# Cross-attention and routed experts on one core: filling turns and last turns in an order of their own, row table ahead of the step tables

## The chip, the cores and the metric

One core of a Trainium2 chip runs the whole program. The metric is the device time in microseconds (us) of one execution. The granted clock is that of TensorE: 1.0 is 2.4 GHz, 0.5 is 1.2 GHz.

## What is computed

There are 16 batches of 128 tokens with 512 numbers each. The attention treats a batch as 128 channels by 512 positions: 8 heads of 16 channels, rotary positions on queries and keys, and a context of the same shape.

```python
x = x + xattn(layernorm(x), ctx)      # q, k, v = W @ inp + b; rotary on q, k
                                      # softmax(q k^T / 4) v; W_o @ out + b_o
t = layernorm(x).reshape(2048, 512)
w, e = top_k(t @ gate_w.T, 8)         # 32 experts, softmax over the 8 chosen
g, u = t @ w_gate_proj[e].T, t @ w_up_proj[e].T       # 192 wide
x = x + sum_k softmax(w)_k * (silu(g) * u) @ w_down_proj[e].T
```

## The kernel before

**Two phases.** The first is a chain of turns, n from -5 to 19, one for each step of a software pipeline over the batches; the second is a loop of up to 160 expert steps, each for one tile of 128 chosen tokens of one expert. Between them VectorE computes a plan of the steps.

**A turn** (`batch_turns`, `turn` of each engine) works on several batches at once: `bl` = n+4 is normalised, `bq` = n+3 gets its projections and rotary positions, `b1` = n+1 its scores for the row maxima, `b2` = n its scores, exponentials and value products, `bo` = n-1 its output and residual, `br` = n-2 its second normalisation, the logits and the choice of experts, and `bs` = n-3 has its rows scattered into the table `expert_rows` in memory. Every engine runs its own list in order, with semaphores between them. Turns -3 to -1 are the filling turns; no batch is in its exponentials yet. In turns 15 and 16 the last two batches drain.

**The way of one batch before its scores.** VectorE takes the statistics (L908 to L914: statistics, aggregation, addition of EPS), GpSimd the power and the shift (L581, L584), ScalarE the normalised x (L731), TensorE four projections in fp32, two records each (L1210 to L1217). VectorE multiplies one pair with the cosines (L905), ScalarE reads the turned pair (L701), GpSimd multiplies it with the sines and adds (L588, L602). ScalarE writes the high fp16 half (L665), GpSimd the low one (L527). SP stores both to memory and loads them back stacked; TensorE's scores for maxima (L1381) and VectorE's maxima, 16 a batch (L899), follow.

**The end of a batch.** ScalarE reads the value products into `o_raw`, in which some rows are the denominators. SP stores these, loads them as 128x32, VectorE inverts them (L919), SP stores them and loads them back spread over the rows, GpSimd multiplies (L595), TensorE makes the output product (L1228), and VectorE adds the residual (L1013).

**The choice of experts.** TensorE's logits (L1247) go to a PSUM bank; VectorE copies them scaled (L939), takes the eight highest (L952), their indices (L957) and casts these (L958), compares them with all expert numbers (L962), sums to a mask (L969), writes weights and token numbers (L977, L978), counts the token number on (L980), and computes the places of the rows (L988 to L998). GpSimd scatters eight rows' columns a batch (L543).

**Banks.** Two pairs of PSUM banks are shared in turn by `m0`, `qk`, `m1` to `m8`, `lg`, `m9` to `m15`, `y` and `cnt`: who comes two places later waits for the one before (`bank_is_free`). The bank of `lg` goes to `m10`.

**Between the phases.** VectorE's plan (L1078 on) gives the step table after 40 instructions; its prefix sum over experts is eleven of them. SP stores and loads the step table, then the table of adds, then waits for the scatters and loads the row table. GpSimd writes four small transfers (L616), waits for the table of adds and starts gathering tokens (L633). ScalarE copies the row numbers (`g_idx`). The first experts' weights are split into halves by `first_weights` in turn 17.

## Time and profile before

| | us |
|---|---|
| median of 3 runs | 1184.73 (1184.3 to 1190.09) |
| the profiled execution | 1200.81 |
| its span, first to last instruction | 1199.0 |

| engine | busy us | share of the span |
|---|---|---|
| TensorE (PE) | 1019.9 | 85% |
| VectorE (DVE) | 726.0 | 61% |
| ScalarE (ACT) | 774.1 | 65% |
| GpSimd (POOL) | 761.8 | 64% |

The span is one execution as the hardware profiler took it, and what lies around it makes the execution's own time. Shares are means over stages with different limits: the rows further down cut the span into stages. PEld is TensorE's weight load, and a name with q (SPq, POOLq) is an engine's queue. An instruction's idle time before it is followed by what ended it.

### The profile page before, as it was taken

What the parts mean: (1) busy time and instruction counts of PE and PEld (TensorE: products, weight loads), DVE (VectorE), ACT (ScalarE), POOL (GpSimd) and SP (SyncE); (2) the same over time, 40 slices, a digit from 0 to 9 for tenths busy, and PEclk for the clock granted to TensorE, in tenths of its full rate; (3) what the DMA queues carried; (4) which work ended last, traced back from release to release, by engine and by line L of the source; (5) the groups of instructions that cost most, each with busy time, mean ns of one, the idle gap of its engine ahead of it and who ended that gap; (6) DMA issues with size and microseconds to landing.
All of it is one profiled execution on the core that took longest, in us unless ns stands there. A gap on an engine that the chain in (4) does not pass through costs nothing.

```text
span 1199.0 us, 29221 instructions
## 1 busy us (share of the span) xinstructions
PE 1019.9 (85%) x6948; PEld 482.1 (40%) x6949; DVE 726.0 (61%) x1453; ACT 774.1 (65%) x1806; POOL 761.8 (64%) x652
## 2 busy tenths in 40 slices
PE   3588998888888898884139999999999999999996
PEld 1222222222222221221026555566566566556663
DVE  2578889989999897862535354554444455444421
ACT  1268878777787785664127666666666676666674
POOL 4523466666666665434656777676777777777776
PEclk8679999999999997887569999999999999999998
DMA  4433434333333332431056878898788898888674
GB/s 138 119 89 112 138 85 121 117 106 116 117 117 116 100 103 77 117 104 34 19 187 156 220 196 213 185 226 213 177 213 212 209 229 196 209 218 203 140 140 89
DMA packets 89700, 176.09 MB, mean 147 GB/s; under 512 B 24340, under 2 KB 41108, under 8 KB 85414
## 3 DMA queue, kind: packets, MB, share of 16 engines
q0 software_dynamic: 38080, 75.58, 29.7%
q1 hardware_dynamic: 51556, 99.80, 26.6%
q8 instruction: 25, 0.41, 0.1%
q14 instruction: 35, 0.29, 0.1%
q10 hardware_dynamic: 4, 0.02, 0.0%
HBM read 118.78 MB, written 61.65 MB: 150 GB/s over the span
## 4 chain that ended last, share of the span: by engine, by line
PE 40%; DVE 21%; issue 15%; DVEq 6%; ACT 6%; ACTq 3%; POOL 2%; DMA 1%; another core or an unknown queue 1%; SPq 0%; POOLq 0%
PE ps L1409 10%; DVE mx L899 10%; PE ps L1370 6%; PE ps L1381 4%; PE ps L1358 4%; DVEq L340 4%; ACTq L340 2%; PE ps L1417 2%; PE ps L1228 2%; DVE w_lo L1159 2%; PE ps L1222 1%; ACT o_raw L665 1%; ACT pr L675 1%; DVE w_hi L1154 1%; POOL expert_rows L543 1%
## 5 line engine op out<-in xcount | busy, mean ns | idle before, releaser
L899 DVE TENSOR_REDUCE mx<-ps 128x2 f32<-128x1024 f32 x256 | 303.3, 1222 | 36.4 <-PE ps L1381 32.9
L675 ACT ACTIVATE pr<-ps 128x512 f32<-128x512 f32 x512 | 279.0, 600 | 63.7 <-PE ps L1358 51.0
L1409 PE MATMUL ps<-w_hi,o_raw 128*128 x1200 | 317.5, 326 | 2.3 <-DVE rope_b L1171 1.8
L649 POOL DMA_INDIRECT out<-v,s_idx x148 | 254.8, 1722 | 100.7 <-issue 43.1
L633 POOL DMA_INDIRECT pr<-normalised_tokens,g_idx x155 | 168.3, 1086 | 58.7 <-issue 24.0
L1409 PE MATMUL ps<-w_lo,o_raw 128*128 x600 | 195.8, 326 | 0.0
L665 ACT ACTIVATE o_raw<-ps 128x1024 f16<-128x1024 f16 (+1 forms) x183 | 175.8, 961 | 2.9 <-PE ps L1370 1.9
L1409 PEld LDWEIGHTS ps<-w_hi,o_raw 128*128 128x128 f16 x1200 | 117.5, 98 | 89.7 <-issue 6.0
L543 POOL DMA_INDIRECT expert_rows<-rows,rowi x128 | 127.3, 995 | 34.7 <-issue 33.1
L1171 DVE SCALAR_TENSOR_TENSOR rope_b<-rope_a,stacks,ps 128x192 f32<-128x192 f32 x150 | 61.8, 412 | 141.6 <-ACT rope_a L787 83.4
L1176 DVE TENSOR_TENSOR rope_s<-rope_b,rope_s 128x128 f16<-128x128 f32 x149 | 43.5, 292 | 170.3 <-issue 115.3
L1370 PE MATMUL ps<-pr,v 128*32 128x512 f32 x1024 | 142.8, 631 | 0.7 <-ACT pr L675 0.6
L1358 PE MATMUL ps<-stacks 49*128 49x512 f16 x512 | 125.7, 398 | 19.7 <-ACT pr L675 15.2
L1381 PE MATMUL ps<-stacks 48*128 48x512 f16 x512 | 107.2, 405 | 38.3 <-DVE mx L899 26.4
L1417 PE MATMUL ps<-ch,pr 128*128 128x128 f16 x1208 | 92.8, 220 | 30.4 <-DMA pr<-normalised_tokens,g_idx 27.9
L581 POOL TENSOR_TENSOR rstd<-vare,cf 128x1 f32<-128x1 f32 x32 | 19.2, 599 | 139.9 <-DVE vare L914 137.8
L787 ACT ACTIVATE rope_a<-ps 128x192 f32<-128x192 f32 x150 | 50.0, 333 | 86.8 <-issue 66.5
L665 ACT ACTIVATE v<-ps 128x512 f32<-128x512 f32 x164 | 98.6, 601 | 8.4 <-PE ps L1222 6.1
L1417 PEld LDWEIGHTS ps<-ch,pr 128*128 128x128 f16 x1208 | 79.7, 98 | 52.1 <-issue 34.1
L1159 DVE SCALAR_TENSOR_TENSOR w_lo<-stage,w_hi x155 | 95.9, 683 | 0.1
L665 ACT ACTIVATE rope_s<-rope_b 128x192 f16<-128x192 f32 x149 | 55.4, 372 | 62.5 <-DVE rope_b L1171 53.3
L665 ACT ACTIVATE x<-ps 128x384 f16<-128x384 f16 x148 | 73.2, 494 | 34.6 <-remote 23.4
(161 smaller groups left out, 1508.8 us busy)
## 6 DMA issues: line engine op xcount, KB each, us to landing
stage<-in_expert_w SPq DMA_DIRECT2D x32, 1280.0 KB
stacks<-qk_parts SPq DMA_DIRECT2D x128, 96.0 KB
w_lo<-in_x SPq DMA_DIRECT2D x32, 256.0 KB, 2.8
w_lo<-in_ctx SPq DMA_DIRECT2D x32, 256.0 KB
qk_parts<-qk SPq DMA_DIRECT2D x32, 256.0 KB
qk_parts<-qk SPq DMA_DIRECT2D x32, 128.0 KB
out<-x SPq DMA_DIRECT2D x16, 256.0 KB
normalised_tokens<-x2s SPq DMA_DIRECT2D x16, 256.0 KB
```

The costliest lines, as they stand in the source:

```text
L543: nc.gpsimd.indirect_dma_start(rows_d, bass.IndirectOffsetOnAxis(rowi[:, b.slot(2), k:k + 1], 0), rows[:, b.slot(2), k, :], None).then_inc ...
L633: nc.gpsimd.indirect_dma_start(xg[:, r, :], None, tok_d, bass.IndirectOffsetOnAxis(g_idx[:, r, 0:1], 0)).then_inc(gathered[r], 16)
L649: nc.gpsimd.indirect_dma_start(out_rows, bass.IndirectOffsetOnAxis(s_idx[:, s.slot(4), 0:1], 0), y_sb[:, s.slot(4), :], None, bounds_check ...
L665: copy = lambda o, i, s=1.0: nc.scalar.activation(o, i, ACT.Copy, scale=s)
L675: nc.scalar.activation(pr[:, n % 8, :], bank(f"s{n}"), ACT.Exp, scale=DH ** -0.5).then_inc(exp_done, 1)
L899: V.tensor_reduce(mx[:, b.slot(2), at:at + 3:2, tile], bank(f"m{n}"), AXX, ALU.max).then_inc(mx_done, 1)
L1159: lo = V.scalar_tensor_tensor(w_lo[:, bass.ds(at_slot + at, LO_PIECE)], stage[:, bass.ds(at_src + at, LO_PIECE)], WSCALE, w_hi[:, bass.ds( ...
L1358: mm(bank(f"s{n}"), k_st[rows_of, b.slot(2), p, sc * P:(sc + 1) * P], q_st[rows_of, b.slot(2), p, :], start=True, stop=True).then_inc(s2_m ...
L1370: last = mm(ps_o[2 * DH * i:2 * DH * (i + 1), :], v1[:, b.slot(2), k % NSC, head, :], pr[:, (4 * k + i) % 8, :], start=(k % NSC == 0), sto ...
L1381: last = mm(bank(f"m{n}")[:, side, :], q_st[rows_of, b.slot(2), p, i * P:(i + 1) * P], k_st[rows_of, b.slot(2), p, :], start=True, stop=True)
L1409: last = mm(ps[:, s.slot(2), 0:2 * INTER], xt[:, s.slot(2), at:at + P], w[:, cols], start=(m == 0), stop=(m == 3 * KT - 1))
L1417: last = nc.tensor.transpose(ps[:, 2 + s.slot(2), :].bitcast(F16)[:, n * P:(n + 1) * P], xg[:, s.slot(GROUP), n * P:(n + 1) * P], ident)
```

## The change

**Loads.** x of batch 0 and the projection weights are SP's first transfers; the other constants follow in turns -4 and -3 with semaphores of their own (`proj_in`, `turn_in`, `consts_in`). The rest of the setup on VectorE, and the bias product on TensorE, move into turn -3. TensorE multiplies zeros 12 times first.

**Filling turns** have lists of their own. In them VectorE makes the whole rotary step and the low halves (`first_rope`, `first_low`) in place of ScalarE's reading, GpSimd's four operations and its two subtractions; ScalarE normalises first. GpSimd stores the empty row table in turn -2 in place of the start, and issues its four small transfers at the start.

**All turns.** The addition of EPS moves to GpSimd, with a constant of its own for the power. The logits are read in PSUM, without a copy; the index search and its cast stand ahead of maximum 9, and `lg_done`, which frees the bank, follows the index search. The token numbers come from a constant table.

**Turns 15 and 16** have lists of their own. The denominators of batches 14 and 15 are spread over the rows by a product with a selecting matrix (`sums`), inverted as 128x512 and multiplied by VectorE (`over_sums`). `first_weights` follows in turn 16, behind the places of batch 14.

**Between the phases.** The prefix sum is one scan. SP waits for the scatters and loads the first part of the row table ahead of the step table and the table of adds, and the rest of it when four gathers have landed. GpSimd waits for the step table ahead of its gathers and for the table of adds ahead of its first add.

```diff
+                if turn_no == -5:
+                    load_x(bi)
+                    sp.dma_start(pw[:, :, :], proj_w).then_inc(proj_in, 16)
+                    return
+                if turn_no == -4:
+                    load_c(bl)
+                    sp.dma_start(pb[:, :], proj_b).then_inc(turn_in, 16)
+                    sp.dma_start(cf[:, :], const_f).then_inc(turn_in, 16)
+                    load_x(bi)
+                    return
+                if turn_no == -3:
+                    load_c(bl)
+                    rest_of_consts()
+                    load_x(bi)
+                    store_stack(bq, 0)
+                    store_stack(bq, 1)
...
+            for p in range(2):
+                sp.wait_ge(rows_stored[p], 16 * TOPK * (NB // 2))
+            sp.wait_ge(s1_mm, 16 * NB)
+            sp.wait_ge(s2_mm, 32 * NB)
+            table = rows_d[0:E * EROWS, :].rearrange("(p r) f -> p (r f)", p=P)
+            first = FIRST_EXPERTS * TILES * 4
+            sp.dma_start(place_of[:, 0:first], table[:, 0:first]).then_inc(first_rows_in, 16)
...
+            for r in range(AHEAD - LEAD):
+                sp.wait_ge(gathered[r], 16)
...
+                if turn_no == NB - 1:
+                    normalised_x2(br)
+                    low_of_x2(br)
+                    scatter_rows(bs, (0, 1, 2))
+                    normalised_x2(bo)
+                    scatter_rows(bs, (3, 4, 5, 6, 7))
+                    low_of_x2(bo)
+                    scatter_rows(br, (0, 1, 2, 3, 4, 5, 6, 7))
+                    return
...
+                if turn_no == NB:
+                    normalised_x2(bo)
+                    scatter_rows(br, (0,))
+                    low_of_x2(bo)
+                    scatter_rows(br, (1, 2, 3, 4, 5, 6, 7))
+                    scatter_rows(bo, (0, 1, 2, 3, 4, 5, 6, 7))
+                    return
...
+                nc.gpsimd.tensor_scalar(vare[:, norm:norm + 1], mv[:, norm, 1:2], EPS, None, ALU.add).then_inc(vare_done[norm], 1)
+                gp.wait_ge(vare_done[norm], b.count(1, 1))
+                apart(gp)
+                nc.gpsimd.tensor_tensor(rstd[:, norm:norm + 1], vare[:, norm:norm + 1], half[:, :], ALU.pow).then_inc(rstd_done, 1)
...
+            gp.wait_ge(tab_in, 16)
...
+                    if bl.live():
+                        normal_x()
+                    if bq.live():
+                        high_of_qk(bq, 0)
+                        high_of_qk(bq, 1)
+                    if b1.live():
+                        read_v(b1)
+                        max_row(b1, 0)
+                    return
...
+            def first_rope(b, w):
+                dve.wait_ge(turn_mm, b.count(2, w + 1))
+                need(dve, rope_sum, b.count(2, w - 1))
+                V.scalar_tensor_tensor(rope_b[:, w, :], bank("kr" if w else "qr"), pb[:, 2 * w + 1:2 * w + 2], cf[:, SIN:SIN + T], ALU.add, ALU.mult).then_inc(turned, 1)
+                dve.wait_ge(rope_done, b.count(2, w + 1))
+                dve.wait_ge(turned, b.count(2, w + 1))
+                need(dve, qk_lo, b.count(2, w - 1))
+                V.tensor_tensor(rope_s[:, w, :], rope_a[:, w, :], rope_b[:, w, :], ALU.add).then_inc(rope_sum, 1)
+            def first_low(b, w):
+                dve.wait_ge(qk_hi, b.count(2, w + 1))
+                need(dve, stack_stored[w], b.count(32, 0))
+                V.tensor_tensor(qk[:, 2 * w + LO, :], rope_s[:, w, :], qk[:, 2 * w + HI, :], ALU.subtract).then_inc(qk_lo, 1)
...
+                link(V.max(top[:, :], bank("lg")[:, 0, 0:E]))
+                V.tensor_scalar(ntop[:, :], top[:, 0:1], -1.0 / WSCALE, None, ALU.mult).then_inc(ntop_done, 1)
+                return link
+            def highest_index(b, link):
+                V.max_index(topi[:, :], top[:, :], bank("lg")[:, 0, 0:E]).then_inc(lg_done, 1)
                 dve.wait_ge(lg_done, b.count(1, 1))
-                apart(dve)
-                link(V.max(top[:, :], lg[:, :]))
-                V.tensor_scalar(ntop[:, :], top[:, 0:1], -1.0, None, ALU.mult).then_inc(ntop_done, 1)
-                return link
-
-            def highest_index(b, link):
-                link(V.max_index(topi[:, :], top[:, :], lg[:, :]))
                 link(V.tensor_copy(topf[:, :], topi[:, :]))
...
+            def over_sums(b, g):
+                n = 2 * (b.count(1) - NB + 2) + g + 1
+                dve.wait_ge(sums_mm, n)
+                dve.wait_ge(on_done, 2 * (NB - 2))
+                V.reciprocal(rcb[:, g, :], v_bank[1][:, g, :]).then_inc(over_done, 1)
+                dve.wait_ge(over_done, n)
+                need(dve, y_mm, b.count(1))
+                V.tensor_tensor(o_n[:, g, :], o_raw[:, b.slot(2), g, :], rcb[:, g, :], ALU.mult).then_inc(on_done, 1)
...
+                if turn_no == NB - 1:
+                    over_sums(bo, 0)
+                    over_sums(bo, 1)
+                    residual(bo)
+                    stats_of_x2(bo)
+                    link = choice(br)
+                    weights(br, link)
+                    read_counts(br)
+                    places(br, link)
+                    over_sums(bo + 1, 0)
+                    return
...
+                if turn_no == NB:
+                    over_sums(bo, 1)
+                    link = choice(br)
+                    residual(bo)
+                    stats_of_x2(bo)
+                    weights(br, link)
+                    read_counts(br)
+                    places(br, link)
+                    first_weights()
+                    return
...
+                    if bq.live():
+                        rope(bq, 0)
+                        rope(bq, 1)
+                        first_rope(bq, 0)
+                        first_rope(bq, 1)
+                    if it.count(1) == -1:
+                        maxima(0, 4)
+                    if bq.live():
+                        first_low(bq, 0)
+                        first_low(bq, 1)
+                    if it.count(1) == -FILL:
+                        rest_of_setup()
+                    if it.count(1) == -1:
+                        maxima(4, 12)
+                    return
...
+            link(V.tensor_tensor_scan(first_step, n_tiles, zero_per_expert, 0.0, ALU.add, ALU.add))
...
+            def sums(b, g):
+                pe.wait_ge(mx_done, 16 * NB)
+                pe.wait_ge(cnt_done, b.count(2, -2))
+                pe.wait_ge(on_done, b.count(2, g - 1))
+                pe.wait_ge(o_read, b.count(2, g + 1))
+                mm(v_bank[1][:, g, :], cf[:, SUMS:SUMS + P], o_raw[:, b.slot(2), g, :], start=True, stop=True).then_inc(sums_mm, 1)
...
+                    s(0)
+                    pv(7)
+                    s(2)
+                    sums(bo, 0)
+                    s(4)
+                    pv(0)
+                    s(6)
+                    sums(bo, 1)
+                    s(8)
+                    pv(1)
+                    s(10)
+                    s(12)
+                    pe.wait_ge(lg_done, NB - 3)
+                    pe.wait_ge(mx_done, 16 * NB)
+                    pe.wait_ge(x2_done, NB - 2)
+                    output(bo)
+                    bank_is_free(pe, it, "xt")
+                    tokens_transposed(br)
+                    pv(2)
+                    s(14)
+                    pe.wait_ge(x2_done, NB - 1)
+                    logits(br)
...
+                if turn_no == NB:
+                    pv(7)
+                    bank_is_free(pe, it, "xt")
+                    tokens_transposed(br)
+                    sums(bo, 1)
+                    pe.wait_ge(lg_done, NB - 2)
+                    logits(br)
+                    bank_is_free(pe, it, "y")
+                    output(bo)
+                    bank_is_free(pe, it, "cnt")
+                    counts_of(br)
+                    return
```

## Rows read from the trace of the kernel before

**Rows 1.** The page's first line.

```profile
span 1199.0 us, 29221 instructions
```

**Rows 2.** Windows by stage: busy us (instructions) per engine, granted clock, DMA share, GB/s.

```profile
0.00:65.14 65.14, 29.82 (x69) 10.83 (x70) 29.50 (x45) 12.77 (x20) 28.89 (x34) 0.75 0.40 125
158.08:435.71 277.63, 242.31 (x1547) 72.09 (x1546) 251.24 (x404) 215.90 (x422) 184.49 (x188) 0.99 0.39 113
524.95:553.87 28.92, 22.92 (x127) 5.75 (x125) 6.50 (x27) 20.58 (x40) 12.31 (x13) 0.82 0.15 45
553.87:619.74 65.87, 8.01 (x60) 4.09 (x58) 32.76 (x118) 8.55 (x17) 40.23 (x41) 0.56 0.21 68
619.74:1199.00 579.26, 553.00 (x4192) 342.61 (x4192) 258.37 (x658) 383.19 (x1046) 419.19 (x299) 0.99 0.80 193
```

**Rows 3.** Timeline of the filling turns: start us, length us, engine, line [idle before <-releaser].

```profile
13.98 2.04 PE L1210 MATMUL ps<-xn,pw 128*128 128x512 f32 x2 [5.82 <-ACT xn L731]
26.78 2.04 PE L1210 MATMUL ps<-xn,pw 128*128 128x512 f32 x2 [6.72 <-issue]
...
44.45 1.22 DVE L899 TENSOR_REDUCE mx<-ps 128x2 f32<-128x1024 f32 x1
```

**Rows 4.** Groups of the first 65.14 us: busy us, mean ns, idle before.

```profile
L908 DVE BATCH_NORM_STATS2 stat<-w_lo 128x6 f32<-128x512 f32 x4 | 2.8, 694 | 24.0 <-DMA w_lo<-in_x 24.0
```

**Rows 5.** Timeline of VectorE in turn 9.

```profile
360.89 0.83 DVE L958 CAST topf<-topi 128x8 f32<-128x8 uint32 x1
371.29 0.15 DVE L914 TENSOR_SCALAR vare<-mv 128x1 f32<-128x1 f32 x1
```

**Rows 6.** Groups of nine steady turns; last row: comparison over the whole run, ns min/median/max.

```profile
L1381 PE MATMUL ps<-stacks 48*128 48x512 f16 x288 | 57.8, 386 | 20.4 <-DVE mx L899 12.2 <-issue 6.2 <-DVE lg L939 0.9
L962 DVE TENSOR_TENSOR chosen<-cf,topf 128x256 f32<-128x256 f32 x9 | 9.4, 1040 | 0.3
L958 DVE CAST topf<-topi 128x8 f32<-128x8 uint32 x9 | 6.4, 711 | 0.3
L962 DVE TENSOR_TENSOR chosen<-cf,topf x16: 424/878/1451, 144.6 to 590.4; 128x256 f32<-128x256 f32 x16
```

**Rows 7.** Window of 5 us in turn 13, columns as in rows 2.

```profile
470.00:475.00 5.00, 4.96 (x19) 0.81 (x19) 2.28 (x2) 2.35 (x5) 3.92 (x5) 0.50 0.28 79
```

**Rows 8.** Timeline of the drain; then power and scatters over the whole run.

```profile
559.24 0.35 DVE L919 RECIPROCAL rcp<-den 128x32 f32<-128x32 f32 x1 [1.65 <-DMA den<-denominators]
575.47 0.69 DVE L1013 TENSOR_TENSOR x<-ps,w_lo 128x512 f32<-128x512 f32 x1 [8.15 <-PE ps L1228]
581.23 2.36 POOL L584 TENSOR_SCALAR shift<-mv,rstd 128x1 f32<-128x1 f32 x1 [0.21 <-POOL rstd L581]
580.63 2.83 DVE L924 SCALAR_TENSOR_TENSOR w_lo<-stage,w_hi 128x2560 f16<-128x2560 f32 x1
593.71 0.17 DVE L998 SCALAR_TENSOR_TENSOR rowi<-topi,at_part 128x8 uint32<-128x8 uint32 x1
600.12 0.38 SPq L477 DMA_DIRECT2D step_table<-stepi  x1
602.05 0.25 SPq L479 DMA_DIRECT2D tab<-step_table  x1
607.18 1.63 POOL L543 DMA_INDIRECT expert_rows<-rows,rowi  x1 [0.30 <-issue]
609.20 2.13 POOL L616 DMA_DIRECT2D started_out<-started  x4 [0.29 <-issue]
610.07 0.34 SPq L507 DMA_DIRECT2D stacks<-expert_rows  x1
619.74 1.86 PE L1417 MATMUL ps<-ch,pr 128*128 128x128 f16 x16 [27.92 <-DMA pr<-normalised_tokens,g_idx]
L581 POOL TENSOR_TENSOR rstd<-vare,cf x32: 549/555/1862, 12.0 to 579.2; 128x1 f32<-128x1 f32 x32
L543 POOL DMA_INDIRECT expert_rows<-rows,rowi x128 | 127.3, 995 | 34.7 <-issue 33.1
```

321 lines of the change are left out of this document (228 added, 93 removed).

## The prediction

> **What bounds the kernel now.** I read the page's first lines first, then the busy time of each engine in stretches cut at the joints of the program, then the groups of the steady turns, and last the timelines around the joints. The profiled execution took 1200.81 us, its span 1199.0 us [rows 1]; the median of the three runs is 1184.73 us, 16 us less. The sum is made against 1200.81 and its difference in us is carried over to the median, since most of the 16 us can lie in the expert steps, which this change leaves alone.
>
> The stretches [rows 2] show three regimes. Up to 65.14 us, where turn 0 starts, no engine is busy half of the time: latency. From 158.08 to 435.71 us lie nine turns of 30.85 us with VectorE at 90% and TensorE at 87%: two engines that wait for each other. From 553.87, where the last value product starts, to 619.74, where the first expert tile is transposed, TensorE works 8 of 66 us: latency again. Then 579 us of expert steps with TensorE at 95%, the same instructions in both kernels. So the change can pay in a fill of 65 us, in 13 steady turns and in a drain of 95 us (turn 15 starts at 524.95).
>
> **The fill, part by part.** VectorE's first work waits for x, which is queued behind the seven constants; it is idle 24.0 us there in total before its statistics [rows 4]. The first projection starts at 13.98 and the second at 26.78 [rows 3]: one turn of the fill costs 12.8 us, because ScalarE's next normalisation stands behind the high halves in its list, and these wait for GpSimd's four rope operations. Turn -1's first maximum starts at 44.45 [rows 3]; sixteen of them, two ropes (1.4) and a stall at the value projection take until 65.14, so 19.3 us without the ropes.
>
> After: x comes first. Statistics can start at about 4 us, but GpSimd now has its fills and the four small transfers ahead (2.13 us for the four [rows 8], which left the drain), so it can answer at about 6.4 us. With the variance, the power and the shift 1.6 us (two short operations, a power of 0.555 [rows 8] and the waits), ScalarE's 0.8 us: first projection at about 9, a gain of 5. The twelve products on zeros lie ahead of it while TensorE waits anyway: no cost. Then VectorE alone carries a turn: statistics 1.1 us and eight operations of 512 columns at 0.69 (the residual add is such a one [rows 8]) with short waits, 7.1 us in place of 12.8. Constants must land for the first rope (x, weights, context and the large table, about 1.5 MB; 5 to 10 us would do it), so turn -3 starts on VectorE near 10, is over with the setup at 18, turn -2 at 25, the ropes of turn -1 at 31 to 32. The sixteen maxima with their stall are 19.3 us as today, the two subtractions among them 1.4: turn 0 at 52, 13 us earlier. Bounds: 8 (constants late, cold projections) and 17. GpSimd's row table fill waits until turn -2 and has all turns to land: nothing.
>
> **The steady turns.** Four instructions leave VectorE's list per turn. The two additions of EPS take 0.15 each [rows 5], 0.22 with the wait, and go to GpSimd, in front of the power; GpSimd is busy 184 of 278 us [rows 2]. ScalarE waits for that chain behind the statistics, so it grows by about 0.25 us, which the shorter list ahead of the statistics gives back. The copy of the logits and the token counter are instructions of the same size as the additions, 0.2 to 0.3 each with their waits. All of this lies around a turn's joint, where TensorE is the later of the two in most turns: I take nothing for it, and at most 1.2 a turn.
>
> What is on the path is the place between maxima 12 and 13: TensorE waits for VectorE's maxima 12.2 us in these nine turns [rows 6]. There the index search (two short instructions, 0.3), its cast (mean 0.711) and the comparison with all experts (mean 1.040, at its shortest 0.424) run one behind the other [rows 6]. The cast took 0.83 at 360.89 [rows 5]; both are long because GpSimd multiplies and subtracts at that time. Search and cast move ahead of maximum 9, beside GpSimd's scatters, where VectorE waits for TensorE in many turns. That takes out about 1.0. Two things give back. The comparison now starts earlier and can meet the GpSimd operation that the cast met: plus 0.2. And the logits' bank is given free after the search instead of after the copy, about 0.6 later; maximum 10's products stand next in TensorE's list and scores and value products behind them. Today TensorE waits there 0.9 us in nine turns for the copy [rows 6]. Plus 0.2, at most 0.6. Net 0.6 a turn, times 13: **8 us**; ends 1 (bank hold at its full price) and 18 (everything counts).
>
> Beside it, a rule. The comparison's long form shows two engines excluding each other: 1.040 in the mean against 0.424. The Trainium skill, page "SBUF — State Buffer", section "Who interferes with whom", has it that an instruction of VectorE with two SBUF inputs, or in a two-port mode, and a GpSimd instruction that reads SBUF lock each other out for a whole instruction. It speaks for the cast's move, and against the place of the first weights' split below. The trace agrees: the power, 0.555 in the median, took 1.862 once, beside the split [rows 8]. If the two did not exclude each other, the drain below would be 3 us shorter.
>
> **The last turns.** Batches 14 and 15 lose the way through memory for the denominators (store, load, reciprocal, store, broadcast) and GpSimd's two multiplications; the residual add of batch 15 starts at 575.47, after VectorE waited 8.15 us for the output product [rows 8], 21.6 after the last value product. New: per half a product with a selecting matrix (1 us, 2 at the lower clock), a reciprocal over 128x512 and a multiplication (0.69). No row has such a reciprocal; the one of 32 columns takes 0.35 [rows 8] and a short instruction of one column 0.15 [rows 5], so 6.2 ns a column and 3.3 us here, as an estimate. Between 0.7 (if it ran like the add) and 5.6 (0.35 times 16). It is on the path once, for batch 15's second half.
>
> From turn 15's start: turn 15 stays at 29 us (three products more on TensorE, fewer waits of ScalarE); VectorE is free in it, busy 6.5 of 28.9 [rows 2]. The second half's sums at +32.4, reciprocal to +35.7, multiplication to +36.4, output product at the lower clock 3.7, residual at about +40.3. Before: 575.47, that is +50.5 [rows 8]. 10 us won. Then statistics, GpSimd's chain, ScalarE's normalisation and high half until +45. GpSimd has one scatter of batch 14 first, which waits for VectorE's places (+44.3), and then the low half. Directly behind the places VectorE splits the first weights (its second half takes 2.83 [rows 8], the first about half of that). Before, that split met the power (1.862 in place of 0.555) and the shift (2.36) [rows 8]. Now it meets the scatter and the low half: I take the same 3 us, so the way from the residual to the last batch's places, 18.2 us today (575.47 to 593.71 [rows 8]), loses only the copy and the counter and some waits, 1.5. Places at +57 instead of +68.8: 12 us. The low half lies about 7 us ahead of them (transposes, copy, logits, choice, counts), at +50.
>
> GpSimd is then the end: today its last scatter starts at 607.18 [rows 8], +82.2. Now 15 scatters follow the low half, each 1.27 from start to start ((127.3 + 34.7) / 128 [rows 8]); the last starts at +67.7: 14.5 won. The plan's scan saves over a microsecond in VectorE's list and nothing on the path. After the scatter lands (2.9), SP loads the row table (610.07 today [rows 8]) and **only then** stores and loads the step table, which took 1.93 from the store's issue to the load's [rows 8] and as much again to land. The order turns: today the step table is in long before the row table, in the new order it comes 1.5 us after it. Against that, the rest of the row table and the weights wait until four gathers have landed, which today share the queues with the first gather: from the row table's load to the first tile are 9.7 us [rows 8], and I take 2 off. The two cancel: first tile at about +80, before +94.8. Drain: **15 us**, ends 6 and 21. What is late next: the rest of the row table, needed from tile 8 on by ScalarE; it lands about when it is asked for, 0 to 2 us.
>
> **Sum.** 13 + 8 + 15 = 36: 1200.8 becomes 1165, the median 1149.
>
> **Rivals.** (1) The turns don't move: the logits' bank costs what the cast's move gives. For it: TensorE is as full as VectorE there. Then 13 + 0 + 14: 1157. (2) The turns take the whole of VectorE's saving, 1.4 a turn, and the fill its upper end: 16 + 18 + 16 = 50: 1135. For it: 12.2 us of waits for maxima. (3) The drain gives only 6, because the split blocks GpSimd's scatters one by one or the step table comes 4 us behind, the fill 10: 10 + 7 + 6 = 23: 1162. (4) The new arrangement of the filling turns does nothing, as the constants come too late for the first rope: fill 4, total 27: 1158. (5) Slower: TensorE's clock. In turn 13, behind a gap in TensorE's work at the turn's start, the granted clock is 0.50 (1.2 GHz) though TensorE is busy 4.96 of 5 us [rows 7]; ten such us cost up to 5, since they hold 5 us of work at the full clock. GpSimd's longer chain sits at just that gap. If it made all 13 turns like this, at 3.5 us each, 46 us would be lost against the 28 won in the fill and the drain: 1203. It decides from 2.2 us a turn. Against it: nine turns run at 0.99 with ScalarE already waiting there.
>
> **Chances.** Forecast 0.52 (own range 1142 to 1156), (1) 0.16, (2) 0.12, (3) 0.08, (4) 0.09, (5) 0.03. The range of 8 in 10 leaves out (5) and the far end of (2) and (3): 1132 to 1165. What a measurement can tell from no change is about 0.5%, 6 us; all cases but (5) lie beyond: faster 0.95, same 0.02, slower 0.03.
>
> **What would show it.** Turn 0's first product at 52 (wrong at 58 or more); distance of turns 30.2 (wrong at 30.8 or under 29.6); in place of 12.2 us of waits for maxima about 7; a new wait of TensorE for the index search; reciprocals of 3.3 us; the low half of the last batch stretched by the split; first tile 80 us after turn 15's start; the expert steps within 4 us of 579.

## Result and profile after

| | before | after |
|---|---|---|
| median (lowest to highest), us | 1187.06 (1184.3 to 1190.09) | 1146.78 (1143.28 to 1158.52) |
| ratio after/before, 95% interval | | 0.9677 (0.96 to 0.9755) |
| profiled execution: time, span, us | 1200.8, 1199.0 | 1158.52, 1156.7 |

The medians differ by 40 us, the profiled spans by 42; 36 were forecast. The prediction, 1149 us, is 2 us above the median; its parts are less exact than its sum. Every stage below is held against one profile of the kernel before, whose execution (1200.8 us) lies 11 us above the longest of its timed runs.

Windows of the changed kernel, columns as in [rows 2]: fill, nine steady turns, turn 15, the rest of the drain, expert steps.

```profile
0.00:52.46 52.46, 30.50 (x82) 10.82 (x83) 40.81 (x59) 9.20 (x14) 10.41 (x26) 0.75 0.54 177
136.94:406.55 269.61, 242.85 (x1551) 71.65 (x1550) 248.39 (x371) 213.88 (x423) 188.80 (x206) 0.97 0.39 115
496.65:532.05 35.40, 28.53 (x133) 7.20 (x131) 19.95 (x38) 21.67 (x42) 16.37 (x21) 0.75 0.15 51
532.05:586.36 54.31, 9.94 (x58) 4.56 (x59) 31.32 (x94) 7.11 (x15) 28.13 (x27) 0.53 0.09 23
586.36:1156.70 570.34, 550.71 (x4192) 341.66 (x4192) 258.16 (x658) 383.23 (x1046) 422.00 (x301) 0.99 0.82 200
```

| stage, us | forecast change | before | after | change |
|---|---|---|---|---|
| start to turn 0's first product | -13 | 65.1 | 52.5 | -12.7 |
| turns 0 to 14 | -8 | 459.8 | 444.2 | -15.6 |
| turn 15's start to first expert tile | -15 | 94.8 | 89.7 | -5.1 |
| expert steps | 0 (within 4) | 579.3 | 570.3 | -8.9 |

**Fill.** Timeline of the changed kernel (start us, length us, engine, line, [idle before]): first projection and first rope of turn -3, the first maximum, and turn 0's first product, a transposition of maxima.

```profile
9.02 1.72 PE L1423 MATMUL ps<-xn,pw 128*128 128x512 f32 x2 [2.32 <-issue]
...
10.87 0.75 DVE L1044 SCALAR_TENSOR_TENSOR rope_a<-ps,pb,cf 128x512 f32<-128x512 f32 x1 [0.28 <-PE ps L1423]
...
31.25 1.22 DVE L1038 TENSOR_REDUCE mx<-ps 128x2 f32<-128x1024 f32 x1
...
52.46 0.37 PE L1455 MATMUL ps<-ident,mx 128*16 128x128 f32 x1 [1.74 <-DVE mx L1038]
```

The first projection stood at 13.98 and the first maximum at 44.45 [rows 3]; now they stand at 9.02 and 31.25.

**Turns.** Groups of the nine steady turns (busy us, mean ns | idle before, with its releasers), then the comparison over the whole run (ns min/median/max), to be held against [rows 6].

```profile
L1681 PE MATMUL ps<-stacks 48*128 48x512 f16 x288 | 58.9, 383 | 14.0 <-DVE mx L1038 11.8 <-DVE topi L1106 2.0
L1112 DVE TENSOR_TENSOR chosen<-cf,topf 128x256 f32<-128x256 f32 x9 | 14.4, 1605 | 0.0
L1108 DVE CAST topf<-topi 128x8 f32<-128x8 uint32 x9 | 2.7, 296 | 0.3
L1112 DVE TENSOR_TENSOR chosen<-cf,topf x16: 412/1078/3040, 131.6 to 557.8; 128x256 f32<-128x256 f32 x16
```

The cast fell from 711 to 296 ns, but the comparison rose from 1040 to 1605: their sum went from 15.8 to 17.1 us in nine turns. And still a turn is 0.9 us shorter (269.61 in place of 277.63 us for nine).

**Drain.** Timeline of the changed kernel's last turns: the output projections of tiles 14 and 15, and, between them, the last reciprocal; the residual of tile 15; a stretched scatter and low half; the last rows' addresses, the last scatter, SyncE's row table and step table, the first expert tile.

```profile
508.50 3.75 PE L1441 MATMUL ps<-o_n,ow 128*128 128x512 f32 x4 [2.12 <-DVE o_n L1161]
...
536.03 3.36 DVE L1158 RECIPROCAL rcb<-ps 128x512 f32<-128x512 f32 x1 [3.37 <-PE ps L1450]
...
540.64 3.78 PE L1441 MATMUL ps<-o_n,ow 128*128 128x512 f32 x4 [4.03 <-DVE topi L1106]
...
544.46 0.69 DVE L1176 TENSOR_TENSOR x<-ps,w_lo 128x512 f32<-128x512 f32 x1 [2.58 <-PE ps L1441]
...
549.52 1.48 POOL L602 DMA_INDIRECT expert_rows<-rows,rowi  x1 [1.16 <-issue]
551.03 2.89 POOL L583 TENSOR_TENSOR x2s<-xn,x2s 128x512 f16<-128x512 f32 x1
...
560.88 0.17 DVE L1150 SCALAR_TENSOR_TENSOR rowi<-topi,at_part 128x8 uint32<-128x8 uint32 x1
...
572.71 0.96 POOL L602 DMA_INDIRECT expert_rows<-rows,rowi  x1 [0.30 <-issue]
...
575.39 0.32 SPq L536 DMA_DIRECT2D stacks<-expert_rows  x1
575.76 0.42 SPq L538 DMA_DIRECT2D step_table<-stepi  x1
...
586.36 1.01 PE L1717 MATMUL ps<-ch,pr 128*128 128x128 f16 x8 [27.14 <-DMA pr<-normalised_tokens,g_idx]
```

### The profile page after: what moved, and what is told of

Its sections match the earlier page's. It is cut to its first block, busy times and chain, and to the rows that moved or that the text cites. A ratio compares the mean times of both kernels' runs of the same rounds, so it can differ in the third digit from the quotient of the medians.

```text
span 1156.7 us, 29289 instructions
## 1 busy us (share of the span) xinstructions
PE 1017.8 (88%) x6968; PEld 479.8 (41%) x6969; DVE 744.1 (64%) x1402; ACT 767.2 (66%) x1800; POOL 744.5 (64%) x663
## 4 chain that ended last, share of the span: by engine, by line
PE 27%; issue 6%; DVEq 5%; DVE 4%; ACTq 3%; DMA 3%; ACT 2%; POOL 0%; POOLq 0%; SPq 0%
PE ps L1709 14%; PE ps L1717 3%; ACTq L351 3%; DVEq L351 3%; PE ps L1735 2%; PE ps L1739 2%; PE ps L1738 2%; PE ps L1737 2%; PE ps L1736 2%; DVE w_lo L1366 1%; DMA pr<-normalised_tokens,g_idx 1%; DVE w_hi L1361 1%; DMA stage<-in_expert_w 1%; DVE rope_b L1378 1%; PE ps L1725 0%
## 5 line engine op out<-in xcount | busy, mean ns | idle before, releaser
L1038 DVE TENSOR_REDUCE mx<-ps 128x2 f32<-128x1024 f32 x256 | 303.5, 1221 | 28.1 <-PE ps L1681 25.7
L1709 PEld LDWEIGHTS ps<-w_hi,o_raw 128*128 128x128 f16 x1200 | 117.5, 98 | 89.7 <-issue 5.9
L1658 PE MATMUL ps<-stacks 49*128 49x512 f16 x512 | 119.2, 395 | 16.4 <-ACT pr L769 15.3
L1717 PE MATMUL ps<-ch,pr 128*128 128x128 f16 x1208 | 93.0, 220 | 29.4 <-DMA pr<-normalised_tokens,g_idx 27.5
L759 ACT ACTIVATE v<-ps 128x512 f32<-128x512 f32 x164 | 97.6, 595 | 12.6 <-PE ps L1435 11.8
L759 ACT ACTIVATE rope_s<-rope_b 128x192 f16<-128x192 f32 x149 | 55.0, 369 | 76.2 <-DVE rope_b L1378 76.1
L1717 PEld LDWEIGHTS ps<-ch,pr 128*128 128x128 f16 x1208 | 79.7, 98 | 51.1 <-issue 32.7
L674 POOL TENSOR_SCALAR vare<-mv 128x1 f32<-128x1 f32 x32 | 7.4, 231 | 132.3 <-DVE mv L1067 131.3
L1658 PEld LDWEIGHTS ps<-stacks 49*128 49x128 f16 x512 | 31.3, 94 | 136.0 <-ACT pr L769 81.5
```

What stands on the lines that cost most here:

```text
L759: copy = lambda o, i, s=1.0: nc.scalar.activation(o, i, ACT.Copy, scale=s)
L1038: V.tensor_reduce(mx[:, b.slot(2), at:at + 3:2, tile], bank(f"m{n}"), AXX, ALU.max).then_inc(mx_done, 1)
L1658: mm(bank(f"s{n}"), k_st[rows_of, b.slot(2), p, sc * P:(sc + 1) * P], q_st[rows_of, b.slot(2), p, :], start=True, stop=True).then_inc(s2_m ...
L1709: last = mm(ps[:, s.slot(2), 0:2 * INTER], xt[:, s.slot(2), at:at + P], w[:, cols], start=(m == 0), stop=(m == 3 * KT - 1))
L1717: last = nc.tensor.transpose(ps[:, 2 + s.slot(2), :].bitcast(F16)[:, n * P:(n + 1) * P], xg[:, s.slot(GROUP), n * P:(n + 1) * P], ident)
```

## Experiments

Every kernel below is the changed one with the edit shown. The kernel before was timed again beside each group of them, on the same chip, so kernels are compared by their ratio to it; microseconds of stages come from one profile each. The stages of all profiles, in us (turns are measured from one turn's second group of maxima, transposed on TensorE, to the next's; "long" counts comparisons of 2.9 us or more in turns 2 to 12):

| kernel | ratio to before (95%) | turn 0 at | turns 0-14 | mean of turns 2-12 | long | turn 15's start to first tile | expert steps |
|---|---|---|---|---|---|---|---|
| before | 1 | 65.1 | 459.8 | 31.0 | 0 | 94.8 | 579.3 |
| changed | 0.968 (0.960-0.976) | 52.5 | 444.2 | 30.0 | 4 | 89.7 | 570.3 |
| changed, again | 0.967 (0.962-0.971) | 50.8 | 448.5 | 30.2 | 5 | 84.9 | 569.6 |
| comparison early | 0.963 (0.956-0.971) | 52.7 | 440.5 | 28.9 | 0 | 85.6 | 576.5 |
| index late | 0.985 (0.977-0.993) | 53.6 | 461.8 | 31.2 | 0 | 84.6 | 576.8 |
| copy only | 0.969 (0.965-0.972) | 50.8 | 448.6 | 29.9 | 0 | 83.8 | 573.1 |
| EPS on VectorE | 0.971 (0.963-0.980) | 50.5 | 446.5 | 29.7 | 0 | 85.6 | 579.4 |
| rope on GpSimd | 0.976 (0.966-0.985) | 53.9 | 447.2 | 29.5 | 0 | 85.5 | 578.7 |
| last turns as before | 0.976 (0.969-0.982) | 50.8 | 441.7 | 29.4 | 2 | 102.6 | 572.5 |
| output late | 0.960 (0.953-0.966) | 50.8 | 446.0 | 29.9 | 5 | 81.8 | 572.2 |
| row table last | 0.959 (0.957-0.961) | 50.9 | 430.8 | 28.7 | 1 | 81.0 | 567.7 |
| three moves | 0.954 (0.951-0.957) | 51.1 | 435.9 | 28.8 | 0 | 76.3 | 574.6 |
| four moves | 0.950 (0.947-0.953) | 52.5 | 442.9 | 29.1 | 0 | 74.5 | 573.5 |
| 2 us away | 0.973 (0.966-0.980) | 52.3 | 458.1 | 30.6 | 0 | 78.2 | 571.7 |

### What is the run's, and what is the change's?

The changed kernel once more, without an edit.

> The changed kernel once more, unaltered, beside the three kernels that follow, so that the stages of the drain are compared on one chip. The first profile of it had: first product of turn 0 at 52.5 us, turns 0 to 14 444.2 us, turn 15's start to the first tile 89.7 us, expert steps 570.3 us. Two kernels of the first group share its drain instruction for instruction and showed 85.6 and 85.5 us there, and 579.4 and 578.7 us of expert steps. Theory: the expert steps' 9 us and the drain's 4 us belong to one execution or one chip and not to the change; then this run shows 576 to 580 us of expert steps, as before the change, and 85 to 86 us of drain. Rival: they are of the change, and 570 and 89.7 us come again.

Turn 15 and the rest of the drain took 84.9 us here: 4.8 of the first profile's 89.7 belong to that execution. Of the expert steps neither reading holds: the changed kernel showed 569.6 again, but two kernels with the same expert steps showed 579.4 and 578.7, and all the others between 567.7 and 576.8. One stage of unchanged instructions moves by 12 us, so the 8.9 us are not evidence for the change; whether some of them belong to it, one profile of before can't tell. Here are turn 15, its part from 516.01 on, and the expert steps of this run; against the first profile turn 15 has the clock at 0.89 in place of 0.75 and is 4.0 us shorter.

```profile
499.31:530.71 31.40, 24.18 (x132) 6.87 (x130) 18.81 (x37) 21.67 (x42) 13.86 (x18) 0.89 0.16 57
516.01:530.71 14.70, 11.01 (x74) 2.54 (x66) 6.80 (x20) 12.23 (x24) 8.62 (x11) 1.00 0.11 38
584.20:1153.80 569.60, 551.81 (x4192) 342.03 (x4192) 259.08 (x658) 381.95 (x1046) 420.28 (x301) 0.99 0.81 200
```

### The turns: where does the comparison wait?

```diff
                     highest_index(br, link)
+                    choose(br, link)
                 maxima(9, 4)
-                if br.live():
-                    choose(br, link)
                 maxima(13, 2)
```

> One move on VectorE, in every turn: the comparison of the logits with the fourth highest (choose) goes from behind the maxima of steps 9 to 12 to a place ahead of them, right behind the column of the index. Theory: in the changed kernel the comparison meets GpSimd's normalisation and low half of x_mid, and is stretched from 0.4 us to a mean of 1.6 us (once 3.0 us); earlier in the turn GpSimd is at its scatters, between which VectorE gets in. Then the nine comparisons of steady turns fall from 14.4 us in sum to under 7 us, TensorE's wait for the maxima falls with them, and a turn takes 0.7 to 1 us less: 10 to 15 us off 1147, so 1132 to 1137. Rival: VectorE pays the same wait at whatever instruction meets GpSimd, the first maximum behind it becomes late instead, and the turns stay at 29.8 us and the kernel at 1147 within 4. A second rival: the comparison ahead of the maxima of steps 9 to 12 makes these late by 0.4 us a turn and costs 3 to 6 us.

Groups of its nine steady turns:

```profile
L1680 PE MATMUL ps<-stacks 48*128 48x512 f16 x288 | 60.3, 383 | 13.8 <-issue 9.0 <-DVE mx L1038 2.9 <-DVE topi L1106 1.3
L1112 DVE TENSOR_TENSOR chosen<-cf,topf 128x256 f32<-128x256 f32 x9 | 3.8, 426 | 0.3
L1108 DVE CAST topf<-topi 128x8 f32<-128x8 uint32 x9 | 2.4, 264 | 0.3
```

The comparison runs at its shortest, 426 ns, in all nine turns; the waits for maxima fell from 11.8 to 2.9 us, and turns 2 to 12 take 28.9 us. The theory's mechanism holds. The 10 to 15 us that it promised for the whole kernel did not show: the ratio is 0.963 against 0.968 (some 5 us), with intervals that overlap, and turns 13 and 14, with the clock at 0.84 and 0.85, took 31.6 and 34.5 us.

What the comparison meets is seen in turn 3 of the second profile of the changed kernel. VectorE and GpSimd side by side, in order of time:

```profile
157.83 1.16 POOL L583 TENSOR_TENSOR qk<-rope_s,qk 128x512 f16<-128x512 f32 x1
158.32 3.29 DVE L1112 TENSOR_TENSOR chosen<-cf,topf 128x256 f32<-128x256 f32 x1
158.94 1.27 POOL L691 TENSOR_TENSOR o_n<-o_raw,rcb 128x512 f32<-128x512 f32 x1
160.16 1.16 POOL L583 TENSOR_TENSOR qk<-rope_s,qk 128x512 f16<-128x512 f32 x1
161.65 2.36 DVE L1038 TENSOR_REDUCE mx<-ps 128x2 f32<-128x1024 f32 x2
```

It is issued 0.5 us into a low half and does not get in at the end of that one (158.99), nor behind the multiplication (160.21); it ends at 161.61, 0.3 us behind the end of the third instruction (161.32), which is about its own shortest time. That turn took 32.2 us.

Put together over the six kernels with the changed turns (changed, changed again, rope on GpSimd, last turns as before, output late, row table last), turns 2 to 12: 66 turns. The 44 with a comparison of up to 1.3 us took 28.7 us in the mean (28.1 to 31.4), three with 1.35 to 1.5 us took 29.5, two with 1.75 and 1.95 took 31.2, and 17 with 2.9 us or more took 31.7 (30.7 to 32.5).

Part of these 31.7 us is TensorE's clock. Here are two turns of the kernel "output late", each with a comparison of 3.02 us:

```profile
253.60:284.27 30.67, 26.50 (x176) 7.89 (x174) 28.97 (x43) 23.72 (x47) 21.30 (x24) 1.00 0.40 124
402.85:435.30 32.45, 28.28 (x176) 8.48 (x174) 28.34 (x41) 23.13 (x46) 20.26 (x21) 0.93 0.31 101
```

Of the 17 turns, the five with the clock at 1.00 all took 30.7 us and the six with 0.92 or 0.93 took 32.5; of the 44 short ones, 38 had 0.99 or 1.00 and took 28.6. So at full clock a long comparison costs 2.1 us, and where the clock falls in that turn, up to 1.8 more.

Identical instructions made 430.8 to 448.5 us of turns 0 to 14. The count of long comparisons, 1 against 5, goes with these two ends, but it is not all: the kernel with the rope on GpSimd had none and took 447.2 us, with 33.5 and 34.0 us for turns 13 and 14 at a clock of 0.85.

### The turns: which part of the change paid?

All that stood behind the maxima of step 12 goes back there, and the copy of the logits with it:

```diff
+                V.tensor_copy(lg[:, :], bank("lg")[:, 0, 0:E]).then_inc(lg_done, 1)
...
-                    highest_index(br, link)
                 maxima(9, 4)
                 if br.live():
+                    highest_index(br, link)
                     choose(br, link)
```

> Undoes one part of the change on VectorE in every turn: the logits are copied from their bank to SBUF again and read from there, and the index of the four highest and its cast go back behind the maxima of steps 9 to 12, beside GpSimd's normalisation. All else is the changed kernel. Theory of the prediction: this was worth 0.7 us a turn (the cast's 0.71 us against about 0.2 us and the copy saved), so the kernel is 8 to 12 us slower than the changed one, 1155 to 1159, with the casts at some 0.7 us again and the comparison, now behind the cast, back near 1.0 us. Rival: the time that VectorE loses to GpSimd only moves between the cast and the comparison (their sum of nine turns, 711 + 1040 ns a turn before against about 300 + 1605 ns after, is the same within 0.2 us), the index's place is worth nothing, and what was gained in the turns came from the other removed instructions at the turn's end: then it is 2 to 4 us slower at most, by the copy alone, 1149 to 1151.

```profile
L1684 PE MATMUL ps<-stacks 48*128 48x512 f16 x288 | 59.7, 385 | 19.8 <-DVE mx L1039 11.4 <-issue 8.3
L1115 DVE TENSOR_TENSOR chosen<-cf,topf 128x256 f32<-128x256 f32 x9 | 9.4, 1046 | 0.3
L1111 DVE CAST topf<-topi 128x8 f32<-128x8 uint32 x9 | 8.5, 946 | 0.3
```

Both expectations were too small. Turns 0 to 14 take 461.8 us, more than before the change: this place takes back all that the turns had gained. The sum of cast and comparison is 17.9 us against 17.1 in the changed kernel, the same within 0.1 us a turn, as the rival had it, and yet the turns are 1 us longer. So what counts isn't the sum but where it lies. The copy was set apart from the index's place:

> Takes apart the kernel with the late index: here only the copy of the logits is back (VectorE copies them from their bank and reads the copy), while the index and its cast keep the changed kernel's place ahead of the maxima of steps 9 to 12. Theory: what counts is how long VectorE is away between the maxima of step 12 and of step 13. It was index, cast and comparison (2.0 us a turn before the change, 2.3 with the late index: turns of 30.3 to 32.4 us), and is the comparison alone now (0.4 to 1.5 us: turns of 28.1 to 29.8; 3.0 us, in about one turn of four: 30.7 to 32.5). Then the copy alone costs at most 0.3 us a turn: turns 0 to 14 take 431 to 450 us as in kernels with the changed turns, against 462 with the late index. Rival: the copy, or the bank of the logits that it frees sooner, is what made the late index slow, and this kernel's turns 0 to 14 take 455 us or more.

448.6 us, at the upper edge of the changed turns' 430.8 to 448.5; its turns 2 to 12 take 29.9 us, inside their 28.7 to 30.2. So the copy doesn't explain the late index, and is worth nothing that can be seen. The additions of EPS were given back to VectorE:

```diff
-                nc.gpsimd.tensor_scalar(vare[:, norm:norm + 1], mv[:, norm, 1:2], EPS, None, ALU.add).then_inc(vare_done[norm], 1)
...
+                V.tensor_scalar(vare[:, norm:norm + 1], mv[:, norm, 1:2], EPS, None, ALU.add).then_inc(sm, 1)
```

> Undoes one part alone, in every turn: the two additions of EPS to the variances are VectorE's again, each right behind its variance, instead of GpSimd's. Theory A: these two short instructions (0.06 and 0.15 us as profiled before) stood in VectorE's tail behind a turn's last maxima, and with the hand over between instructions they were worth 0.3 to 0.5 us a turn: 5 to 8 us slower than the changed kernel, 1152 to 1155, and TensorE's waits of kind issue ahead of the steps' products come back in part. Theory B, as the prediction had it: they cost VectorE 0.2 us a turn and hold nothing that the turn's end waits for, so the kernel is the same within 3 us, and in filling turns VectorE has the longer turn by 0.2 us. Either way the gain from one turn to the next shows in the distance of the turns' first products, 29.8 us in the changed kernel.

446.5 us, inside the same band: theory B. The token counter was not undone by itself. The last question was whether the time away alone makes a turn long, or the meeting with GpSimd. To the three moves (below) this was added:

```diff
                 maxima(9, 4)
+                if br.live():
+                    for n in range(4):
+                        V.tensor_reduce(spare[:, n, :], chosen[:, :, :].rearrange("p k e -> p e k"), AXX, ALU.add)
                 maxima(13, 2)
```

> A size changed on purpose, on the kernel with three moves: between the maxima of step 12 and of step 13 VectorE does four reductions of 0.58 us more (the sum over the choices, into a tile that nobody reads). The comparison stays ahead of step 9's maxima, so no instruction there waits for GpSimd: reductions of this kind never did in any profile (0.58 to 0.60 us each). VectorE is away from the maxima for some 2.2 us there, as long as index, cast and comparison were before the change (2.0) and with the late index (2.3). Theory: the time away alone sets the turn, whatever fills it: turns 2 to 12 take 30.3 to 32.4 us as in those two kernels, where three moves gave 28.0 to 29.8, turns 0 to 14 take 458 to 468 us instead of 436, and the ratio to the kernel before is 0.972 to 0.982. Rival: it is the meeting with GpSimd (GpSimd delayed by VectorE, and ScalarE's and TensorE's inputs with it) that makes a turn long; then 2.2 us of undisturbed work cost what VectorE's idle time in a turn can't take, under 1 us: turns at 28.5 to 30, turns 0 to 14 in 436 to 450 us, ratio 0.953 to 0.966.

Timeline of one turn's reductions between the maxima, groups of its steady turns (the window is a little short of nine), then turns 4 and 5:

```profile
161.76 2.15 DVE L1248 TENSOR_REDUCE spare<-chosen 128x32 f32<-128x256 f32 x4
163.81 2.37 DVE L1039 TENSOR_REDUCE mx<-ps 128x2 f32<-128x1024 f32 x2
```

```profile
L1248 DVE TENSOR_REDUCE spare<-chosen 128x32 f32<-128x256 f32 x32 | 17.1, 596 | 0.0
L1113 DVE TENSOR_TENSOR chosen<-cf,topf 128x256 f32<-128x256 f32 x9 | 3.8, 425 | 0.3
L1684 PE MATMUL ps<-stacks 48*128 48x512 f16 x282 | 58.2, 384 | 18.6 <-DVE mx L1039 16.5 <-DVE topi L1107 2.0
```

```profile
168.10:199.89 31.79, 28.20 (x175) 8.44 (x174) 28.56 (x47) 23.95 (x47) 20.99 (x23) 0.95 0.37 111
199.89:230.19 30.30, 26.70 (x175) 7.89 (x174) 28.10 (x45) 23.83 (x47) 20.35 (x23) 1.00 0.36 104
```

458.1 us and 0.973: the theory. With no comparison beside GpSimd, four undisturbed reductions bring TensorE's waits for maxima to 16.5 us (3.5 in nine turns with three moves) and the turns to 30.6 in the mean. The clock has its part here too: eight of these eleven turns had it at 1.00 and took 30.1 us, three had 0.95 and took 31.8, while with three moves all eleven had 1.00 and took 28.8. The Trainium skill, page "SBUF — State Buffer", section "Who interferes with whom", says that on trn2 a reduction never meets GpSimd at the shared ports; the trace agrees, with 571 to 629 ns for all 56 of them.

Side by side, VectorE's time away between maxima 12 and 13 and the mean turn: nothing, 28.8 to 29.1 us; the comparison at up to 1.3 us, 28.7; four reductions (163.81 - 161.76 = 2.05 us), 30.6; before (0.3 + 0.71 + 1.04), 31.0; index late (0.3 + 0.95 + 1.05), 31.2; the comparison at 3.0, 31.7. Some 1.3 us are free, and beyond them more than the extra length is paid. At full clock a turn takes 28.6 us up to there, 30.1 at 2.05 and 30.7 at 3.0; what the means have above that is the clock. That the turns at 2.05 us lie 0.4 apart (30.6 and 31.0) shows what is left for all other causes.

### The fill: VectorE's rope, or the order?

Filling turns take the rope from ScalarE and GpSimd again, in the new order:

```diff
+                    if bq.live():
+                        rope_sin(bq, 0)
+                        rope_add(bq, 0)
+                        rope_sin(bq, 1)
+                        rope_add(bq, 1)
+                        low_of_qk(bq, 0)
+                        low_of_qk(bq, 1)
...
-                        first_rope(bq, 0)
-                        first_rope(bq, 1)
```

> Only the filling turns differ from the changed kernel: rotary embedding by ScalarE and GpSimd, as in the kernel before, the new order of the filling turns' other work kept. It tells VectorE's rope from the reordering. Theory: VectorE's rope carries most of the 12.7 us by which turn 0's first product came earlier (65.1 to 52.5 us from the start), since GpSimd's four multiplications and additions a turn stood in the path: turn 0's first product falls back to 60 to 64 us and the kernel to 1155 to 1158. Rival: the reordering (projection ahead of the rest, the first norms ahead of constants, masks later) carries it, the first product of turn 0 stays at 52 to 56 us and the kernel within 4 us of 1147. Turns 0 to 16 and the drain are instruction for instruction those of the changed kernel, so a difference in them is what one run differs from another by.

Its second and third turn's first rope instruction, the third turn's first projection, and its first maximum:

```profile
20.11 0.75 DVE L1057 SCALAR_TENSOR_TENSOR rope_a<-ps,pb,cf 128x512 f32<-128x512 f32 x1
...
27.65 2.04 PE L1431 MATMUL ps<-xn,pw 128*128 128x512 f32 x2 [7.79 <-DMA w_lo<-in_ctx]
...
30.58 0.75 DVE L1057 SCALAR_TENSOR_TENSOR rope_a<-ps,pb,cf 128x512 f32<-128x512 f32 x1
...
33.90 1.23 DVE L1051 TENSOR_REDUCE mx<-ps 128x2 f32<-128x1024 f32 x1 [0.97 <-PE ps L1689]
```

The rival: turn 0 at 53.9 us. The rest of the new fill brings 11.2 of the 12.7 without VectorE's rope: 5.0 of them are there at the first projection (13.98 to 9.02), behind the new order of the loads; the lists of the filling turns, the setup's place and the loads of the later turns were not taken apart from each other. The first maximum is 2.7 us later than with VectorE's rope, of which the two subtractions that no longer stand among the maxima give 1.2 back. In the changed kernel the rope's first instructions stand at 10.87, 20.01 and 26.59; here the third turn's stands at 30.58, and its projection had waited 7.79 us for the load of the context. Kernels with VectorE's rope have turn 0 at 50.5 to 53.6, so the rope is worth 0.3 to 3.4 us.

### The drain

```diff
-                if turn_no == NB - 1:
-                    over_sums(bo, 0)
-                    over_sums(bo, 1)
-                    residual(bo)
...
```

(and likewise in the lists of the other engines: the general lists with their tests run turns 15 and 16.)

> Undoes the last turns alone: turns 15 and 16 run the general lists with tests, the denominators go to memory and come back at every turn, the split of the first expert's weights stands in turn 17 as before, and the row table's first part is still loaded ahead of the step tables. Filling turns and turns 0 to 14 are those of the changed kernel. Theory: the written-out last turns give 7 to 10 us between turn 15's start and the first tile (94.8 us before, 85.6 in the changed kernel), so this kernel shows 93 to 97 us there and is 8 to 11 us slower than the changed one. Rival: the changed kernel's 3.4 us reciprocals (four in sum) and its longer turn 15 eat what the saved trip through memory gives, and the stretch is 86 to 89 us, within 3 us of the changed kernel.

The milestones behind turn 15's start, in us:

| kernel | last value product | residual of tile 15 | its rows' addresses | last scatter | first tile | last scatter to tile |
|---|---|---|---|---|---|---|
| before | 28.9 | 50.5 | 68.8 | 82.2 | 94.8 | 12.6 |
| forecast | 29 | 40.3 | 57 | 67.7 | 80 | 12.3 |
| changed | 35.4 | 47.8 | 64.2 | 76.1 | 89.7 | 13.6 |
| changed, again | 31.4 | 42.9 | 59.3 | 71.1 | 84.9 | 13.8 |
| last turns as before | 33.9 | 56.0 | 74.6 | 88.9 | 102.6 | 13.7 |
| output late | 28.4 | 39.8 | 56.2 | 68.1 | 81.8 | 13.7 |
| row table last | 31.6 | 43.0 | 59.4 | 71.2 | 81.0 | 9.8 |
| three moves | 26.8 | 38.3 | 54.8 | 66.5 | 76.3 | 9.8 |
| four moves | 27.1 | 38.6 | 52.9 | 64.8 | 74.5 | 9.7 |

102.6 us, more than the theory had: 5 of them are turn 15 at a lower clock than in before's profile (0.60 against 0.82; 33.9 us against 28.9), the rest of its chain is that of before within 0.5 us up to the addresses. The ratios, 0.976 against 0.967, put the written-out last turns at 11 us of 1190, with intervals that touch.

**Turn 15.** In the changed kernel TensorE waits 2.12 us for the output projection, which then takes 3.75 us, in both profiles alike. The 4.0 us between them lie behind it: in the first profile the clock falls a second time within the turn, in the second it does not (its 516.01 to 530.71 above has 1.00).

```profile
521.35:532.05 10.70, 8.74 (x27) 1.34 (x26) 5.47 (x12) 5.66 (x13) 6.10 (x7) 0.50 0.08 25
```

Six other kernels with this order of turn 15 (comparison early, index late, copy only, EPS on VectorE, rope on GpSimd, row table last) took 30.9 to 31.7 us for it; so some 31.4 us is its usual length, and 35.4 is that execution's. What made the clock fall twice there is open. Against the wait, the output projection was moved behind the next product:

```diff
                     s(12)
-                    pe.wait_ge(lg_done, NB - 3)
-                    pe.wait_ge(mx_done, 16 * NB)
-                    pe.wait_ge(x2_done, NB - 2)
-                    output(bo)
...
                     s(14)
+                    pe.wait_ge(lg_done, NB - 3)
+                    pe.wait_ge(mx_done, 16 * NB)
+                    pe.wait_ge(x2_done, NB - 2)
+                    output(bo)
...
                     s(18)
+                    pe.wait_ge(x2_done, NB - 1)
+                    logits(br)
```

> One move on TensorE in turn 15: tile 14's output projection goes behind step 14's product and tile 15's logits behind step 18's product, both otherwise as in the changed kernel. In the changed kernel TensorE waited 2.1 us in turn 15 for the divided o of tile 14 and ran the projection at half clock (3.75 us), and turn 15 took 35.4 us against 29 to 30 of the others. Theory: with steps ahead of it the wait is covered, the clock stays up, turn 15 takes 31 to 33 us and the kernel is 2 to 5 us faster than the changed one. Rival: turn 15's length is set by VectorE, whose two reciprocals of 3.4 us stand ahead of maxima, so that the wait comes back ahead of another product: within 1.5 us of the changed kernel. Third: the residual and with it the chain of tile 14 is late by the moved projection, and it is 1 to 3 us slower.

(The logits that are moved are those of tile 13.) Its first 15 us of turn 15, and the output projection in them:

```profile
496.77:511.77 15.00, 12.90 (x76) 3.64 (x76) 11.83 (x17) 11.71 (x22) 5.23 (x7) 1.00 0.25 90
509.07 1.98 PE L1441 MATMUL ps<-o_n,ow 128*128 128x512 f32 x4
```

No wait, and 1.98 us in place of 3.75: full clock. Turn 15 takes 28.4 us in place of 31.4 and 35.4, and the chain then meets the forecast of every milestone up to the last scatter within 0.8 us.

**The row table's place.**

```diff
-            for p in range(2):
-                sp.wait_ge(rows_stored[p], 16 * TOPK * (NB // 2))
...
-            sp.dma_start(place_of[:, 0:first], table[:, 0:first]).then_inc(first_rows_in, 16)
...
             sp.dma_start(before_tab[:, :], before_d[0:STEPS + SEEN, :].rearrange("(o s) f -> o (s f)", o=1)).then_inc(before_in, 16)
             sp.wait_ge(tab_in, 16)
+            for p in range(2):
+                sp.wait_ge(rows_stored[p], 16 * TOPK * (NB // 2))
...
+            sp.dma_start(place_of[:, 0:first], table[:, 0:first]).then_inc(first_rows_in, 16)
```

> One move on SyncE: the load of the row table's first part goes back behind the step tables (store, load, store, load), as in the kernel before. In the changed kernel the step tables' data were written at 565.6 us, but SyncE stood before the row table, which waits for the last scatter, until 575.4, and the load of the step table left at 578.1, the gather's index came at 581.2. Theory: the step tables are in by about 570 us, and the row table alone, 575.4 plus its landing of some 2 us, sets the gather: 2 to 4 us faster than the changed kernel, both between the last scatter and the first tile and in all. Rival, the change's reason: the row table is what the first gather waits for, its first part would go out behind the step table's four transfers by 1 to 2 us later, and the kernel is 1 to 2 us slower.

SyncE's issues in it, and the first tile:

```profile
545.90 0.38 SPq L531 DMA_DIRECT2D step_table<-stepi  x1
...
555.39 0.35 SPq L545 DMA_DIRECT2D stacks<-expert_rows  x1
...
562.67 1.01 PE L1717 MATMUL ps<-ch,pr 128*128 128x128 f16 x8 [23.27 <-DMA pr<-normalised_tokens,g_idx]
```

The step table is stored 9.5 us ahead of the row table, and the last scatter to the first tile takes 9.8 us, 4.0 less than in the changed kernel and 2.8 less than before. So the turned order costs 4.0 us. All else that the change did there is worth 2.8: the first load became smaller, the rest waits behind the gathers, and GpSimd's four small transfers left the place. These were not taken apart.

**Three and four moves.** Comparison early, output late and row table last together; and with them the split of the first expert's weights taken out of turn 16. The edit puts it into turn 15, behind the choice of tile 13, and not, as the expectation says, into turn 16 behind the choice of tile 14:

```diff
                     link = choice(br)
+                    first_weights()
...
                     places(br, link)
-                    first_weights()
```

> Three moves at once on the changed kernel: the comparison ahead of the maxima of steps 9 to 12, the row table's first part loaded behind the step tables, and in turn 15 the output projection behind step 14 and the logits behind step 18. Theory: their gains add up, since they lie in different places: no comparison of 3 us and turns of 28.4 to 29.7 us where the clock is full (turns 0 to 14 in 427 to 441 us), 31 to 32 instead of 35 us or less for turn 15, and 4 us less from the last scatter to the first tile (9.8 instead of 13.8), so turn 15's start to the first tile in 77 to 79 us. Ratio to the kernel before 0.945 to 0.955, where the changed kernel has 0.967. Rival: the comparison ahead of those maxima costs in the last turns or with another execution's clock what it saves, and the ratio is 0.957 to 0.96, that of the single moves on SyncE and TensorE.

> The three moves of the run before and a fourth: VectorE splits the first expert's weights in turn 16 right behind the choice of tile 14, instead of behind tile 14's places at the turn's end, where the split (1.5 and 2.8 us) stands beside GpSimd's low half of tile 15 (2.9 us instead of 1.2) and a scatter. Theory: the split then runs beside TensorE's output projection of tile 15, for which VectorE waits 2.5 us anyway, and the low half is short again: the last batch's places and the first tile come 1.5 to 3 us earlier than with three moves, 75 to 77 us behind turn 15's start. Rival: the split's 4.3 us are longer than VectorE's wait of 2.5, so the residual of tile 15 is late by 1.8 us and all behind it: same as with three moves within 1 us, or up to 2 us slower.

Three moves are at 0.954; singly they gave 0.004, 0.007 and 0.008 off 0.967, only the last of them clear of the changed kernel's second interval, and would give 0.948 if they added up in full. Both kernels, 0.954 and 0.950, are clear of the changed kernel's 0.967, and four moves have the lowest ratio here, though not clear of three. Between them only the milestones tell: the residual is 0.3 us later, the addresses 1.9 earlier. The split started at 513.56, 18.2 us into turn 15, so the expectation's rival, a split longer than VectorE's wait ahead of tile 15's residual, was not put to the test. GpSimd beside it, in the kernel with four moves:

```profile
538.95 1.08 POOL L602 DMA_INDIRECT expert_rows<-rows,rowi  x1 [1.17 <-issue]
540.06 1.16 POOL L583 TENSOR_TENSOR x2s<-xn,x2s 128x512 f16<-128x512 f32 x1
```

The scatter and the low half are at 1.08 and 1.16 us, where they took 1.48 and 2.89 beside the split.

## Why the prediction was right in sum and not in its parts

**Fill: -13 forecast, -12.7 and -14.4 (second profile) measured.** First projection at about 9 (9.02), maxima from 31 to 32 (31.25), turn 0 at 52 (52.46): right. But the step that gave the 12.8 us of a filling turn to GpSimd's rope was wrong as a cause: with that rope and all else of the new fill a turn takes 9.0 and 10.5 us (rope instructions at 11.16, 20.11 and 30.58), against 9.1 and 6.6 with VectorE's, and turn 0 comes only 1.5 us later. The loads and the order of the lists were most of the constraint, VectorE's rope a small addition.

**Turns: -8 forecast, -11 to -16 in two profiles of the kernel, -13 to -29 in the four others with the same turns.** The place was right, the gap behind maxima 12, and so were the nothings: EPS and copy are not seen. Two terms were mis-sized, in opposite directions. "Plus 0.2" for the comparison that meets the cast's GpSimd operation was 0.6 (1605 against 1040 ns) and 1.1 in the second profile (2129): it meets up to three operations in a row. And the gap was priced in proportion, 1.0 us out of it for 1.0 us of the turn, less 0.4 given back; in fact a turn with a gap of up to 1.3 us is 2.3 us shorter (28.7 against 31.0) and one with a gap of 3.0 is 0.7 longer, partly by the clock. The mean of this mixture, 30.0 and 30.2, is near the forecast of 30.2 by luck. The forecast that waits for maxima would fall to about 7 us failed: 12.2 became 11.8 and 15.5; what went were waits of kind issue, 6.2 us in [rows 6]. The index search's price for the logits' bank was right: 2.0 us of waits in nine turns in place of the copy's 0.9, which is 0.1 a turn more (forecast 0.2).

**Drain: -15 forecast, -5.1 and -9.9 measured.** The reciprocal is 3.36 us as estimated (3.3). The way from the last value product to the residual was sized right (11.3; measured 12.4 and 11.5), and so was that to the addresses (16.7; 16.4 and 16.4), with the split in the way as told: priced at 3 us, it stretched one scatter by 0.5 and the low half by 1.7, and taking it away gave 1.9. The step that failed is "turn 15 stays at 29 us": VectorE's two reciprocals in it hold up tile 14's output projection, TensorE waits 2.1 us and comes out at half clock, and the turn took 31.4 us, and 35.4 in the first profile, where the clock fell once more. With that projection two steps later the turn takes 28.4 and the forecast's own numbers appear. The second failure is "the two cancel": the row table's order costs 4.0 us and the rest of the change there gives 2.8. In the second profile the 4.9 us by which 84.9 lies above the forecast's 80 are 2.4 of turn 15, 1.5 behind the last scatter and 1.0 on the ways between; in the first profile turn 15 alone is 6.4 of 9.7.

**Expert steps.** "Within 4 us of 579" was wrong for the profile (570.3), and no step of the change explains it; the same instructions took 567.7 to 579.4. Without these 9 us the profiled execution would have been at 1167, near the 1165 of the sum, so 36 us were forecast and 33 found. That the sum came out so near is luck: the turns gave more than their forecast and the drain less, and the expert steps' 9 us, which no term of the prediction had, are in the 42 us of the spans.

**Rivals.** (5), the clock, did not come for whole stretches of the steady turns (0.97 against 0.99), but it takes up to 1.8 us of a turn with a long comparison. In turn 15, where the forecast left it as it was (0.82), it was 0.75 in one profile and 0.89 in the other. Of (3) the step table behind the row table is what happened, at 4 us, but the split did not block the scatters one by one, and the drain gave 10 in the second profile; in the first it gave 5.1, less than the 6 of this rival. (2) asked for 18 us in the turns by the whole of VectorE's saving, of which the copy and EPS turned out to be worth nothing that can be seen; the best of the six profiles, 430.8 us with one long comparison, gave 29 all the same. (1) falls with the late index, which undoes the turns' whole gain of 15 us and more. (4) falls with turn 0 at 50.8 and 52.5.

## What to carry to other kernels

When two engines wait for each other by turns, find how long one may be away at each point before the other runs dry, and put work there up to that and no more; here 1.3 us are free and 2.05 cost 1.7, of which 1.3 at full clock. Before pricing a wait, look at the granted clock of the turns that have it and of those that don't. An operation that can wait for another engine belongs beside work of that engine that doesn't exclude it, and its price is read from its distribution (0.41, 1.1, 3.0 us), not its mean. When a queue is put in a new order, ask which of its entries has its data last: that one goes last.

## What was not expected of the hardware

VectorE's comparison did not get its turn at the end of the GpSimd instruction that it met: it ended only behind three back-to-back ones, 3.29 us for 0.43 of work. The Trainium skill, page "SBUF — State Buffer", section "Who interferes with whom", speaks of blocking for the whole of one instruction; here the trace shows more. And a VectorE reciprocal over 512 columns takes 3.36 us, over 32 columns 0.35 [rows 8], where an addition of 512 takes 0.69.
